# Two bias vectors added to rows in SBUF: by GpSimd instructions, or by accumulating transfers from GpSimd's queue

## The chip, the cores and the metric

One core of one Trainium2 chip runs the kernel, in one launch. The metric is the device time of an execution in microseconds, and a kernel's time is the median over its runs. The engines: TensorE (PE) multiplies matrices, VectorE (DVE) and ScalarE (ACT) do elementwise work, GpSimd (POOL) does some too and issues transfers from a queue of its own, SyncE (SP) issues most transfers. They share an on-chip memory of 128 partitions (SBUF). PE writes its products to eight banks of PSUM. Engines wait for each other by semaphores only.

## The reference

The input x has 64 blocks of 32 rows by 512 columns, float32. Four layers of the form x = x + ffn(cond(x)) follow one another. Cut to what matters here:

```
x = x + ffn0(cond0(x))    # cond: a 32x32 mix for each block; ffn0: silu(gate) * up, then down, 1792 wide
x = x + ffn1(cond1(x))    # cond1: grouped convolution, 9 taps, along the 512 columns
x = x + ffn2(cond2(x))    # top 8 of 64 experts' bias rows, mixed, and the row scaled
x = x + ffn3(cond3(x))    # x * in_scale @ sign(W).T * out_scale + bias, scales from a softmax routing

def ffn1(c):
    combine = top2(softmax(c @ W_router.T))
    lora = einsum(einsum(c, A_stack) * combine, B_stack) * 2
    return c @ W_base.T + b_base + lora

def ffn3(c):
    routing = softmax(c @ gate_w.T)
    return c * (routing @ in_channel_scale) @ sign(weight).T * (routing @ out_channel_scale) + bias
```

The change is about b_base of layer 1 (512 numbers, bbase in the kernel) and bias of layer 3 (512 numbers, bias3). Both are the same for all 2048 rows of x.

## The kernel before

x lives in SBUF as x_all, 128 partitions by 16 tiles of 512 columns. A group g is four tiles (GT = 4), so there are four groups, and each layer runs over groups 0 to 3. Nothing schedules the work: each engine's program is written out by hand, runs in the order of the code, and waits where a wait_ge stands. PE turns a group's tiles into cT (cond), DVE adds the cond's bias, PE multiplies cT by the layer's weights into PSUM banks, and DVE or GpSimd adds the result to x_all.

**Layer 1.** Its convolution needs other rows beside each other, so layer 0's result takes a way through DRAM. GpSimd's part copies each tile into two halves (L446), SP writes them to y_dram (put_back, L316), and SP reads them back as stg, 16 transfers for each group (regroup, L308). PE's conv takes stg, DVE turns and adds (cond1), and PE makes the router's logits and the low-rank product (lora_a_router), then the product with wbase (base), then lora_b. Group 1's conv comes behind group 0's base on PE and waits for group 1's stg. DVE's residual(1, g) adds the four banks to x_all, and ahead of its first addition waits until base_bias(g) is done. base_bias(g) (L457 to L461) is one GpSimd instruction that adds bbase to the four tiles of group g. base_bias(0) stands behind the wait for all 16 parts and for the weights of layer 1; the other three stand behind the splitting of layer 2's and 3's weights (eb_lo, in_w, out_w), in a loop.

**Layer 3.** For each group DVE's route3 makes the routing weights: a multiply into ex, two casts into rcat (L1167), two subtractions into rcat. PE turns rcat (turn_routing, L769) and makes from it the scales (in_scales, out_scales). DVE scales cT, ACT and DVE and GpSimd split it into high and low parts: GpSimd's split_x (L496) makes the even low parts, c_lo or c_lo_odd. PE's sign_product(g, j) takes them. DVE's scale_out multiplies the product by the output scale into t1. GpSimd adds the layer's bias to x_all (bias_3, L499 to L501, one instruction for four tiles) and then t1 (finish_3, L508, one for each tile), and SP stores the tile. GpSimd's order in this layer is block_diagonal(3, 1), split_x(0), bias_3(0), and then for g = 0, 1, 2: block_diagonal(3, g + 2), bias_3(g + 1), three tiles of finish_3(g), split_x(g + 1), the last tile of finish_3(g). bias_3(g) waits until PE has read x_all for cond of group g.

bbase and bias3 come from DRAM as tiles of 128 partitions by 512, issued by SP beside the other weights.

Of the kernel before, what the change touches and what calls it, by code (L numbers as in the profile page):

```python
# [17 lines left out]
ALU = mybir.AluOpType  # L18
# [3 lines left out]
P = 128  # L22
D = 512
# [29 lines left out]
def build(nc, A, out):  # L53
    ctx = ExitStack()
    with ctx:
        def sb(name, shape, dt=F32):
            return ctx.enter_context(nc.sbuf_tensor(name, shape, dt))

        def sem(name):
            return ctx.enter_context(nc.semaphore(name))  # L60
# [65 lines left out]
        with ExitStack() as first:  # L126
            def sb1(name, shape):
                return first.enter_context(nc.sbuf_tensor(name, shape, F32))

            war = sb1("war", [P, S, AR])  # L130
            wbase = sb1("wbase", [P, S, D])
            wlb = sb1("wlb", [P, D])
            bbase = sb1("bbase", [P, D])
            hm = sb1("hm", [P, GT, P])
            hmT = sb1("hmT", [P, TOK])
# [9 lines left out]
        wsg = sb("wsg", [P, S, D])  # L145
        bias3 = sb("bias3", [P, D])
        inc3 = sb("inc3", [P, D])
# [85 lines left out]
        s_hmT = sem("s_hmT")  # L233
        s_base_bias = sem("s_base_bias")

# [27 lines left out]
        s_scaled_lo_odd = sem("s_scaled_lo_odd")  # L263
        s_bias3 = sem("s_bias3")
        s_rescaled = sem("s_rescaled")
# [11 lines left out]
        WLOADS = 16 * 2 * CB * Q  # L277
        LOADS1 = 16 * 10


        @block.sync
        def _(sp):
# [66 lines left out]
            for n in range(4):  # L349
                at, h, to = n * ROWS, n // 2, n % 2  # L350
                rows = slice(h * WIN + to, (h + 1) * WIN, 2)
                for dst, src in ((war, "war"), (wbase, "wbase")):
                    sp.dma_start(dst[at:at + ROWS], A[src][rows]).then_inc(s_weights1, 16)
            for dst, src in ((bbase, "bbase"), (wlb, "wlb")):
                sp.dma_start(dst[:], A[src]).then_inc(s_weights1, 16)
            sp.wait_ge(s_up, G * M)
            for dst, src in ((eb2, "eb2"), (inc3, "inc3"), (outc3, "outc3"), (wsg, "wsg"),
                             (wr2, "wr2"), (rb2, "rb2"), (wr3, "wr3"), (bias3, "bias3")):
                sp.dma_start(dst[:], A[src]).then_inc(s_weights23, 16)
# [19 lines left out]
        def _(pool):  # L379
# [77 lines left out]
            def base_bias(g):  # L457
                pool.wait_ge(s_weights1, LOADS1)
                xg = x_all[:, ds(g * GT, GT), :]
                pool.tensor_tensor(xg, xg, bbase[:].unsqueeze(1).broadcast_to([P, GT, D]),  # L460
                                   ALU.add).then_inc(s_base_bias, 1)  # L461

            pool.wait_ge(s_parted, NT)
            base_bias(0)
            pool.wait_ge(s_weights23, 16 * 8)
            pool.wait_ge(s_w_hi, 4)
            half = P // 2
            pool.wait_ge(s_base_bias, 1)
            pool.tensor_tensor(eb_lo[:], eb2[:], eb_hi[:].bitcast(F32), ALU.subtract).then_inc(s_w_lo, 1)
            pool.wait_ge(s_w_lo, 1)  # L470
            for n, (w, src) in enumerate(((in_w, inc3), (out_w, outc3))):
                pool.tensor_tensor(w[half:P], src[half:P], w[half:P].bitcast(F32), ALU.subtract).then_inc(s_w_lo, 1)
                pool.wait_ge(s_w_lo, n + 2)
            with pool.Fori(1, G) as g:
                base_bias(g)

# [21 lines left out]
            def bias_3(g):  # L498
                pool.wait_ge(s_cond_mm[3], S * (g + 1))  # L499
                xg = x_all[:, g * GT:(g + 1) * GT, :]  # L500
                pool.tensor_tensor(xg, xg, bias3[:].unsqueeze(1).broadcast_to([P, GT, D]), ALU.add).then_inc(s_bias3, 1)  # L501

            def finish_3(g, js):
                pool.wait_ge(s_bias3, g + 1)
                for j in js:
                    pool.wait_ge(s_rescaled, g * GT + j + 1)
                    xg = x_all[:, g * GT + j, :]
                    pool.tensor_tensor(xg, xg, t1[:, j], ALU.add).then_inc(s_x_new[3], 1)  # L508
# [18 lines left out]
        def _(pe):  # L527
# [155 lines left out]
            def layer1(g, more):  # L683
                base(g)
                pe.wait_ge(s_hm, g + 1)
                if more:
                    for q in range(Q - 1):
                        conv(g + 1, q)
                    pe.wait_ge(s_turned1, Q * (g + 1) + 1)
                    turn_hm(g)  # L690
                    conv(g + 1, Q - 1)
                    lora_b(g)
                    lora_a_router(g + 1)
                else:
                    cond(2, 0, SPARING, [nothing, nothing, nothing, lambda: (turn_hm(g), pe.wait_ge(s_cT[2], 1))])
                    lora_b(g)
                    pe.wait_ge(s_w_lo, 3)
                    pe.wait_ge(s_weights23, 16 * 8)
                    router2(0)
                pe.wait_ge(s_x_new[1], GT * (g + 1))  # L700
# [127 lines left out]
        def _(act):  # L828
# [48 lines left out]

            act.wait_ge(s_weights23, 16 * 8)
            act.wait_ge(s_product[0], G * GT)
# [58 lines left out]
        def _(dve):  # L938
# [160 lines left out]
            dve.wait_ge(s_set, 3)  # L1099
            with dve.Fori(0, G - 1) as g:  # L1100
                route1(g)
                cond1(g + 1)
                dve.wait_ge(s_base_bias, g + 1)
                residual(1, g)
            route1(G - 1)
            cond(2, 0, SPARING)
            dve.wait_ge(s_base_bias, G)
            residual(1, G - 1)
# [107 lines left out]

            dve.wait_ge(s_bias3, G)
            dve.wait_ge(s_rescaled, NT)
# [91 lines left out]
```

## Time and profile before

| | |
|---|---|
| median of 3 runs | 581.22 us (581.1 to 581.5) |
| the profiled execution | 581.92 us |
| its span, first to last instruction | 579.9 us |
| mean granted TensorE clock | 0.983 |
| PE busy | 549.5 us, 95% of the span |
| DVE busy | 263.1 us, 45% |
| ACT busy | 134.1 us, 23% |
| GpSimd busy | 186.7 us, 32% |
| moved by DMA | 50.32 MB, mean 87 GB/s |

The profile is one execution. Its page lists busy time by engine, the span in 40 slices, the chain of work that ended last, and groups of instructions by line with what they waited for. The trace behind it can be asked for one engine's timeline, for its waits, and for the busy time of all engines in a stretch of time. Layer 0 takes the time up to about 342 us, layer 1 to about 455, layer 2 to about 505, layer 3 the rest. A granted clock of 1.00 is TensorE's 2.4 GHz, 0.50 is 1.2 GHz. The DMA share of a stretch is the mean busy share of 16 DMA engines; packets of one engine can overlap, so it can pass 1.

### The profile page before, as it was taken

Reading aid. Unit: us, or ns where it says so; the run is one execution under the profiler, and the core shown is the slowest. Engines: PE = TensorE matmul, PEld = TensorE weight load, DVE = VectorE, ACT = ScalarE, POOL = GpSimd, SP = SyncE. Lnnn points to the kernel's source line nnn. Section 1 sums busy time; section 2 is a strip of 40 time slices with the busy share of each in tenths; the row PEclk is TensorE's granted clock in tenths of the full one; section 3 lists DMA queues with packets and bytes.
Section 4 is the critical chain, followed back from the end, with each engine's and each line's share of the span. In section 5 each row is a group of like instructions: output and inputs, shape, how many; then the busy total and the mean of one; then the engine's idle time right before and its main releaser. Section 6 shows DMA issues by size and latency. Waiting matters only on the chain.

```text
span 579.9 us, 7213 instructions
## 1 busy us (share of the span) xinstructions
PE 549.5 (95%) x2689; PEld 421.6 (73%) x2689; DVE 263.1 (45%) x529; ACT 134.1 (23%) x230; POOL 186.7 (32%) x152
## 2 busy tenths in 40 slices
PE   7999999999999999999999998699999999886996
PEld 5788888888888888888888863254455889764774
DVE  4542254522227222245222264435262687767775
ACT  4322223222223222232222221101010132232232
POOL 2699981200002100012000008600000155466986
PEclk9999999999999999999999999699999999997999
DMA  9398230490000400003050059494910343110412
GB/s 303 134 419 312 50 93 0 107 176 24 0 0 32 131 0 0 0 0 92 1 128 1 0 193 172 65 144 57 178 18 1 90 114 86 19 18 1 139 62 109
DMA packets 84211, 50.32 MB, mean 87 GB/s; under 512 B 69600, under 2 KB 74464, under 8 KB 83424
## 3 DMA queue, kind: packets, MB, share of 16 engines
q1 hardware_dynamic: 82096, 38.97, 30.8%
q0 software_dynamic: 2016, 11.01, 5.3%
q8 instruction: 12, 0.20, 0.1%
q10 hardware_dynamic: 80, 0.08, 0.0%
q14 instruction: 7, 0.06, 0.0%
HBM read 31.93 MB, written 8.62 MB: 70 GB/s over the span
## 4 chain that ended last, share of the span: by engine, by line
PE 82%; DVE 9%; DMA 4%; SPq 2%; issue 2%; POOL 1%; ACT 1%; DVEq 0%; POOLq 0%
PE ps L529 80%; DMA xs<-in_x 2%; SPq L308 2%; DVE cT L940 1%; DVE rcat L1167 1%; DMA stg<-y_dram 1%; POOL x_all L483 1%; DVE rest L1122 1%; DVE x_all L940 1%; DMA y_dram<-prod 1%; PE ps L769 1%; DVE lg L940 1%; DVE c_lo L940 0%; DVE ex L940 0%; DVE t L940 0%
## 5 line engine op out<-in xcount | busy, mean ns | idle before, releaser
L529 PE MATMUL ps<-c_lo,wl 128*128 128x512 f32 x448 | 172.9, 390 | 0.4 <-POOL c_lo L408 0.3
L529 PE MATMUL ps<-c_hi,wl 128*128 128x512 f32 x448 | 173.1, 390 | 0.2
L940 DVE TENSOR_TENSOR hff<-silu,ps 128x512 f32<-128x512 f32 x56 | 38.5, 688 | 163.2 <-PE ps L529 163.1
L529 PEld LDWEIGHTS ps<-c_lo,wl 128*128 128x128 f32 x448 | 84.1, 188 | 18.6 <-POOL c_lo L408 0.7
L529 PEld LDWEIGHTS ps<-c_hi,wl 128*128 128x128 f32 x448 | 84.1, 188 | 18.1 <-ACT c_hi L830 0.8
L529 PE MATMUL ps<-wl,h_hi 128*128 128x512 f32 x224 | 87.7, 391 | 0.0
L529 PE MATMUL ps<-wl,h_lo 128*128 128x512 f32 x224 | 87.2, 389 | 0.0
L940 DVE TENSOR_TENSOR h_lo<-hff,h_hi 128x512 fp32r<-128x512 f32 x56 | 46.1, 823 | 39.1 <-ACT h_hi L830 39.1
L408 POOL TENSOR_TENSOR c_lo<-cT,c_hi 128x512 fp32r<-128x512 f32 x8 | 10.7, 1343 | 158.1 <-ACT c_hi L830 158.1
L830 ACT ACTIVATE h_hi<-hff 128x512 fp32r<-128x512 f32 x56 | 35.4, 632 | 112.5 <-DVE hff L940 112.5
L864 ACT ACTIVATE silu<-ps 128x512 f32<-128x512 f32 x56 | 33.5, 598 | 116.4 <-PE ps L529 116.4
L529 PE MATMUL ps<-wbase,cT 128*128 128x512 f32 x128 | 55.6, 592 | 0.0
L529 PEld LDWEIGHTS ps<-wl,h_hi 128*128 128x128 f32 x224 | 42.1, 188 | 10.4 <-issue 1.7
L529 PEld LDWEIGHTS ps<-wl,h_lo 128*128 128x128 f32 x224 | 42.1, 188 | 8.6
L529 PEld LDWEIGHTS ps<-wbase,cT 128*128 128x128 f32 x128 | 24.0, 190 | 28.7 <-issue 28.7
L940 DVE TENSOR_TENSOR cT<-ps,bias_bc 128x512 f32<-128x512 f32 x48 | 31.3, 684 | 19.4 <-PE ps L529 19.1
L446 POOL COPY prod<-x_all 128x512 f32<-128x512 f32 x16 | 10.1, 647 | 92.9 <-DVE x_all L940 84.8
L416 POOL TENSOR_TENSOR blk<-agg,pack_c 128x512 f32<-128x512 f32 x11 | 11.4, 1041 | 78.3 <-PE ps L529 78.3
L529 PEld LDWEIGHTS ps<-blk,xs 128*128 128x128 f32 x256 | 31.5, 201 | 3.1 <-DMA xs<-in_x 1.8
L529 PE MATMUL ps<-blk,xs 128*128 128x128 f32 x256 | 32.7, 286 | 0.2 <-DMA xs<-in_x 0.2
L483 POOL TENSOR_TENSOR x_all<-x_all,t 128x512 f32 (+1 forms) x16 | 20.0, 1285 | 29.7 <-ACT t L895 29.7
L991 DVE STREAM_TRANSPOSE tr<-ps 128x512 f32<-128x512 f32 x16 | 11.3, 712 | 36.6 <-PE ps L529 36.5
(155 smaller groups left out, 651.5 us busy)
## 6 DMA issues: line engine op xcount, KB each, us to landing
wl<-in_wl POOLq DMA_DIRECT2D x14, 768.0 KB, 10.0
stg<-y_dram SPq DMA_DIRECT2D x64, 128.0 KB, 4.9
xs<-in_x SPq DMA_DIRECT2D x4, 1024.0 KB, 7.9
x_all<-in_x SPq DMA_DIRECT2D x1, 4096.0 KB, 14.5
y_dram<-prod SPq DMA_DIRECT2D x16, 256.0 KB, 2.3
xs<-x_all SPq DMA_DIRECT2D x4, 1024.0 KB, 4.9
out_x<-x_all SPq DMA_DIRECT2D x16, 256.0 KB, 2.0
bias_bc<-bias_dram SPq DMA_DIRECT2D x15, 256.0 KB, 5.0
```

The source lines that it names most:

```text
L308: sp.dma_start(stg[dt * ROWS:(dt + 1) * ROWS, q, :, at:at + WIN], src.rearrange("b p c -> p b c")).then_inc(s_staged[1], 16)
L408: pool.tensor_tensor(c_lo[:, s], cT[:, s], c_hi[:, s].bitcast(F32), ALU.subtract).then_inc(s_c_lo_even, 1)
L416: pool.tensor_tensor(blk[:].rearrange("p j (b o) -> p j b o", b=TB), agg[:, COND[l], ds(g * GT, GT)].unsqueeze(2).broadcast_to([P, GT, TB, ...
L446: pool.tensor_copy(halves_x[:, j % 2], x_all[:, j, :].rearrange("p (s c h) -> p h s c", s=S, h=2)).then_inc(s_parted, 1)
L483: pool.tensor_tensor(xg, xg, t1[:, j:j + 1, :], ALU.add).then_inc(s_t1_added, 1)
L529: return pe.matmul(o, l, r, start=start, stop=stop)
L769: ins = pe.transpose(bank(5)[:, cols(j)], rcat[:, j], ident)
L830: return act.activation(o, i, ACT.Copy)
L864: act.activation(silu[:, m % 2], bank(4 + 2 * (m % 2)), ACT.Silu).then_inc(s_silu, 1)
L940: return dve.tensor_tensor(o, a, b, op)
L991: dve.transpose(tr[:, q % 2], bank(4 + q)).then_inc(s_turned1, 1)
L1122: ins = dve.match_replace(rest[:, j], m8[:, j], logit[:, j], LOWEST)
```

## The change

base_bias(g) and bias_3(g) become DMA issues on GpSimd's queue. Each reads the bias vector from DRAM, where it lies as 128 rows of 512, repeats it over four tiles, and adds it to x_all in SBUF (accum_op). The SBUF tiles bbase and bias3 go, and so do the loads that filled them. Each of the eight transfers has a semaphore of its own, which rises by 16 when it has landed. All four base_bias are issued in a row once all 16 parts are made, and no longer wait for layer 1's weights. The bias_3 issues stand where the additions stood. DVE's loop over groups of layer 1 is written out, since its wait is for another semaphore in each group; the instructions in it are the same.

```diff
-            bbase = sb1("bbase", [P, D])
-        bias3 = sb("bias3", [P, D])
-        LOADS1 = 16 * 10
+        LOADS1 = 16 * 9
...
             def base_bias(g):
-                pool.wait_ge(s_weights1, LOADS1)
-                xg = x_all[:, ds(g * GT, GT), :]
-                pool.tensor_tensor(xg, xg, bbase[:].unsqueeze(1).broadcast_to([P, GT, D]),
-                                   ALU.add).then_inc(s_base_bias, 1)
+                pool.dma_start(x_all[:, g * GT:(g + 1) * GT, :], A["bbase"].unsqueeze(1).broadcast_to([P, GT, D]),
+                               accum_op=ALU.add).then_inc(s_base_bias[g], 16)
 
             pool.wait_ge(s_parted, NT)
-            base_bias(0)
-            pool.wait_ge(s_weights23, 16 * 8)
+            for g in range(G):
+                base_bias(g)
+            pool.wait_ge(s_weights23, 16 * 7)
             pool.wait_ge(s_w_hi, 4)
             half = P // 2
-            pool.wait_ge(s_base_bias, 1)
...
-            with pool.Fori(1, G) as g:
-                base_bias(g)
...
             def bias_3(g):
                 pool.wait_ge(s_cond_mm[3], S * (g + 1))
-                xg = x_all[:, g * GT:(g + 1) * GT, :]
-                pool.tensor_tensor(xg, xg, bias3[:].unsqueeze(1).broadcast_to([P, GT, D]), ALU.add).then_inc(s_bias3, 1)
+                pool.dma_start(x_all[:, g * GT:(g + 1) * GT, :], A["bias3"].unsqueeze(1).broadcast_to([P, GT, D]),
+                               accum_op=ALU.add).then_inc(s_bias3[g], 16)
 
             def finish_3(g, js):
-                pool.wait_ge(s_bias3, g + 1)
+                pool.wait_ge(s_bias3[g], 16)
...
-            with dve.Fori(0, G - 1) as g:
+            for g in range(G - 1):
                 route1(g)
                 cond1(g + 1)
-                dve.wait_ge(s_base_bias, g + 1)
+                dve.wait_ge(s_base_bias[g], 16)
                 residual(1, g)
```

GpSimd's order at the seam of layers 0 and 1, from its last part of x (COPY) to the loop of layer 2, before the change (the row of L460 behind the branch is in a loop of three):

```order
L446 COPY prod<-x_all 128x512 [waits s_y1]
L460 TENSOR_TENSOR x_all<-x_all,bbase 128x2048 [waits s_weights1,s_parted]
L469 TENSOR_TENSOR eb_lo<-eb,eb_hi 128x512 [waits s_base_bias,s_w_hi,s_weights23]
L472 TENSOR_TENSOR in_w<-inc,in_w 64x512 [waits s_w_lo]
L472 TENSOR_TENSOR out_w<-outc,out_w 64x512 [waits s_w_lo]
L474 UNCONDITIONAL_BRANCH [waits s_w_lo]
L460 ISA [waits s_weights1]
L460 TENSOR_TENSOR x_all<-x_all,bbase 128x2048
```

and after it:

```order
L443 COPY prod<-x_all 128x512 [waits s_y1]
L455 DMA x_all<-in_bbase 128x4x512 [waits s_parted]
L455 DMA x_all<-in_bbase 128x4x512 x3
L464 TENSOR_TENSOR eb_lo<-eb,eb_hi 128x512 [waits s_w_hi,s_weights23]
L467 TENSOR_TENSOR in_w<-inc,in_w 64x512 [waits s_w_lo]
L467 TENSOR_TENSOR out_w<-outc,out_w 64x512 [waits s_w_lo]
```

The three base_bias that came behind the splitting of the weights now come ahead of it, beside the first, and all of them are transfers.

GpSimd's order in layer 3, from the even low parts of group 0 (c_lo) to those of group 1 (c_lo_odd), before the change:

```order
L496 TENSOR_TENSOR c_lo<-cT,c_hi 128x512 [waits s_scaled_hi] x2
L501 TENSOR_TENSOR x_all<-x_all,bias 128x2048 [waits s_cond_mm3]
L416 TENSOR_TENSOR blk<-agg,pack_c 128x512 [waits s_cond_mm3]
L501 TENSOR_TENSOR x_all<-x_all,bias 128x2048 [waits s_cond_mm3]
L508 TENSOR_TENSOR x_all<-x_all,t 128x512 [waits s_rescaled,s_bias3]
L508 TENSOR_TENSOR x_all<-x_all,t 128x512 [waits s_rescaled] x2
L496 TENSOR_TENSOR c_lo_odd<-cT,c_hi_odd 128x512 [waits s_scaled_hi] x2
```

and after it:

```order
L489 TENSOR_TENSOR c_lo<-cT,c_hi 128x512 [waits s_scaled_hi] x2
L493 DMA x_all<-in_bias 128x4x512 [waits s_cond_mm3]
L413 TENSOR_TENSOR blk<-agg,pack_c 128x512 [waits s_cond_mm3]
L493 DMA x_all<-in_bias 128x4x512 [waits s_cond_mm3]
L501 TENSOR_TENSOR x_all<-x_all,t 128x512 [waits s_rescaled,s_bias3_0]
L501 TENSOR_TENSOR x_all<-x_all,t 128x512 [waits s_rescaled] x2
L489 TENSOR_TENSOR c_lo_odd<-cT,c_hi_odd 128x512 [waits s_scaled_hi] x2
```

No row has changed its place here. The two additions of the bias are issues, and the first finishing addition waits for the semaphore of group 0's transfer, where it waited for an instruction of its own engine.

## Rows read from the trace of the kernel before

**Rows 1.** The page's chain that ended last, share of the span by line

```profile
PE ps L529 80%; DMA xs<-in_x 2%; SPq L308 2%; DVE cT L940 1%; DVE rcat L1167 1%; DMA stg<-y_dram 1%; POOL x_all L483 1%; DVE rest L1122 1%; DVE x_all L940 1%; DMA y_dram<-prod 1%; PE ps L769 1%; DVE lg L940 1%; DVE c_lo L940 0%; DVE ex L940 0%; DVE t L940 0%
```

**Rows 2.** PE's waits: who for whom, total us, times, longest us

```profile
PE ps L769 <- DVE rcat L940: 7.8, 4, 5.1
```

**Rows 3.** Timelines of SP and PE, layer 1: start us, us, work [idle before]

```profile
350.51 12.20 SPq L308 DMA_DIRECT2D stg<-y_dram  x16
...
367.33 5.39 PE L529 MATMUL ps<-stg,wconv 128*64 128x512 f32 x12 [7.38 <-DMA stg<-y_dram]
```

**Rows 4.** Timeline of DVE in layer 3, route3 of groups 0, 1 and 2

```profile
508.16 0.19 DVE L940 TENSOR_TENSOR ex<-ex,stat 128x32 f32<-128x32 f32 x1
508.39 0.27 DVE L1167 CAST rcat<-ex 128x32 fp32r<-128x32 f32 x2
508.69 0.42 DVE L940 TENSOR_TENSOR rcat<-ex,rcat 128x32 f32<-128x32 f32 x2
...
520.86 0.72 DVE L940 TENSOR_TENSOR ex<-ex,stat 128x32 f32<-128x32 f32 x1
521.61 4.51 DVE L1167 CAST rcat<-ex 128x32 fp32r<-128x32 f32 x2
526.16 1.36 DVE L940 TENSOR_TENSOR rcat<-ex,rcat 128x32 f32<-128x32 f32 x2
...
543.82 0.79 DVE L940 TENSOR_TENSOR ex<-ex,stat 128x32 f32<-128x32 f32 x1
544.64 1.28 DVE L1167 CAST rcat<-ex 128x32 fp32r<-128x32 f32 x2
```

**Rows 5.** Timeline of GpSimd in layer 3

```profile
515.42 5.11 POOL L501 TENSOR_TENSOR x_all<-x_all,bias 128x2048 f32<-128x2048 f32 x1
...
521.49 4.51 POOL L501 TENSOR_TENSOR x_all<-x_all,bias 128x2048 f32<-128x2048 f32 x1
...
532.29 1.28 POOL L496 TENSOR_TENSOR c_lo_odd<-cT,c_hi_odd 128x512 fp32r<-128x512 f32 x1 [1.59 <-ACT c_hi_odd L830]
...
539.98 4.58 POOL L501 TENSOR_TENSOR x_all<-x_all,bias 128x2048 f32<-128x2048 f32 x1
544.52 1.27 POOL L508 TENSOR_TENSOR x_all<-x_all,t 128x512 f32<-128x512 f32 x1
```

**Rows 6.** Timeline of PE in layer 3

```profile
527.57 1.11 PE L769 MATMUL ps<-pack_c,rcat 128*128 128x128 f32 x4 [5.14 <-DVE rcat L940]
...
539.28 1.08 PE L529 MATMUL ps<-sgn,c_lo_odd 128*128 128x512 f32 x4
...
546.43 0.66 PE L769 MATMUL ps<-pack_c,rcat 128*128 128x128 f32 x4 [1.05 <-DVE rcat L940]
...
561.91 0.66 PE L769 MATMUL ps<-pack_c,rcat 128*128 128x128 f32 x4 [0.32 <-DVE rcat L940]
```

**Rows 7.** Stretches: us, busy us (x) by engine, PEclk, DMA share, GB/s

```profile
527.50:534.80 7.30, 7.14 (x21) 5.51 (x22) 3.59 (x7) 2.42 (x4) 3.78 (x3) 0.60 0.01 2
546.40:551.00 4.60, 4.48 (x20) 3.35 (x21) 3.53 (x6) 2.33 (x4) 3.82 (x3) 1.00 0.42 159
```

**Rows 8.** DMA: x_all's load; xs issued at 73.4; weights; first xs load

```profile
x_all<-in_x SPq DMA_DIRECT2D x1, 4096.0 KB, 14.5
...
DMA to landing us min/median/max: 7.5/7.5/7.5
...
L385 POOL DMA_DIRECT2D wl<-in_wl x2: 541/630/719, 4.7 to 5.4; - x2
...
DMA to landing us min/median/max: 7.6/8.3/9.1
...
2.13 12.12 DMA xs<-in_x
```

**Rows 9.** Line L460, min/median/max ns; then GpSimd's waits

```profile
L460 POOL TENSOR_TENSOR x_all<-x_all,bbase x4: 4492/4508/4546, 350.1 to 368.1; 128x2048 f32 x3, 128x2048 f32<-128x2048 f32 x1
...
POOL blk L416 <- PE ps L529: 78.3, 1, 78.3
```

**Rows 10.** A stretch ahead of group 1's conv (columns as in rows 7)

```profile
362.00:365.00 3.00, 0.00 (x0) 0.00 (x0) 0.00 (x0) 0.00 (x0) 3.00 (x2) 0.62 1.42 149
```

More of the change, by code:

```diff
@@ L233, in build @@
         s_hmT = sem("s_hmT")
-        s_base_bias = sem("s_base_bias")
+        s_base_bias = [sem(f"s_base_bias{g}") for g in range(G)]
         s_w_hi = sem("s_w_hi")
@@ L263, in build @@
         s_scaled_lo_odd = sem("s_scaled_lo_odd")
-        s_bias3 = sem("s_bias3")
+        s_bias3 = [sem(f"s_bias3_{g}") for g in range(G)]
         s_rescaled = sem("s_rescaled")
@@ L353, in _ @@
                     sp.dma_start(dst[at:at + ROWS], A[src][rows]).then_inc(s_weights1, 16)
-            for dst, src in ((bbase, "bbase"), (wlb, "wlb")):
-                sp.dma_start(dst[:], A[src]).then_inc(s_weights1, 16)
+            sp.dma_start(wlb[:], A["wlb"]).then_inc(s_weights1, 16)
             sp.wait_ge(s_up, G * M)
             for dst, src in ((eb2, "eb2"), (inc3, "inc3"), (outc3, "outc3"), (wsg, "wsg"),
-                             (wr2, "wr2"), (rb2, "rb2"), (wr3, "wr3"), (bias3, "bias3")):
+                             (wr2, "wr2"), (rb2, "rb2"), (wr3, "wr3")):
                 sp.dma_start(dst[:], A[src]).then_inc(s_weights23, 16)
@@ L697, in layer1 @@
                     pe.wait_ge(s_w_lo, 3)
-                    pe.wait_ge(s_weights23, 16 * 8)
+                    pe.wait_ge(s_weights23, 16 * 7)
                     router2(0)
@@ L875, in _ @@
             layer0(G - 1, False)
-            act.wait_ge(s_weights23, 16 * 8)
+            act.wait_ge(s_weights23, 16 * 7)
             act.wait_ge(s_product[0], G * GT)
@@ L1106, in _ @@
             cond(2, 0, SPARING)
-            dve.wait_ge(s_base_bias, G)
+            dve.wait_ge(s_base_bias[G - 1], 16)
             residual(1, G - 1)
@@ L1215, in _ @@
             scale_out(G - 1, range(GT))
-            dve.wait_ge(s_bias3, G)
+            dve.wait_ge(s_bias3[G - 1], 16)
             dve.wait_ge(s_rescaled, NT)
```

## The prediction

> **What bounds the kernel now.** Read the chain of work that ended last first: PE's matmuls hold 80% of it and no DMA or GpSimd line is above 2% [rows 1]. So an edit to GpSimd and DMA counts only where PE stands idle. Then ask where PE waits. Two waits matter for this change. In layer 3 PE waits 7.8 us in four places for rcat, the routing weights that DVE writes, and 5.1 us of that in one place [rows 2]. At the start of layer 1's second group (group 1) it waits 7.38 us for stg, the regrouped rows that SP's transfers bring from DRAM, 16 of which were issued in 12.20 us [rows 3].
>
> **Why the long wait for rcat.** Set DVE's rows of layer 3 beside GpSimd's [rows 4, 5]. The same small steps run once for each group. In group 0 the multiply takes 0.19 us, the two casts 0.27, the two subtractions 0.42. In group 1 they take 0.72, 4.51 and 1.36: 5.71 us more. GpSimd's addition of bias3 to four tiles runs from 521.49 for 4.51 us, exactly over the casts. In group 2 the multiply and the casts take 0.79 and 1.28, 1.61 us more. GpSimd's addition of 539.98 to 544.56 lies on the first, and the finishing addition right behind it (1.27 us) on the second. Without the long one the finishing addition comes some 4 us earlier, ahead of DVE's steps. So I read the two engines as taking turns. The additions held DVE's work back.
>
> **Layer 3, what goes.** The four additions of 4.51 to 5.11 us leave GpSimd and its place is taken by four DMA issues. PE's waits are 5.14, 1.05 and 0.32 us in groups 1, 2 and 3 [rows 6]. The first two are shorter than what DVE gets back (5.71 and 1.61). The third I count with them, as the same kind of collision. That is 6.51 us. What is left of the 7.8 us, 1.3 us in group 0, has nothing of GpSimd in it (DVE's steps are the short ones there) and stays. The clock comes on top. After the 5.14 us of idling PE's granted clock is 0.60 over the stretch from the routing turn to the next cond product. The same stretch of group 2, whose wait was only 1.05 us, has 1.00 and lasts 4.6 us instead of 7.3 [rows 7]. Without the long wait those 2.7 us go too, unless some other gap lets the clock fall. Layer 3's upper bound is 6.5 + 2.7 = 9.2 us.
>
> **Layer 3, what comes.** Now finish_3(0), GpSimd's addition of t1 to group 0's rows, must wait until a transfer has landed. Queued behind it on GpSimd is split_x(1), which makes the even low parts for sign_product(1, 0) on PE, and behind that everything of group 2. Before, PE took the low parts at 539.28 [rows 6]. With 5.14 + 2.70 us gone it would want them at 531.4, and the second even one some 0.5 us later. GpSimd has to do three finishing additions of 1.27 us and two splittings of 1.28 first [rows 5], 6.4 us, so the bias must be there by 525.5. The issue is made when the additions' place comes, at 515.42 [rows 5]. So there are 10.1 us from issue to landing. The trace has no accumulating transfer. The nearest rows are an xs load of 1024 KB, the same size in rows of the same 2 KB, at 7.5 us, and x_all's load of 4096 KB at 14.5 us, 3.6 us for each megabyte [rows 8]. If the transfer costs no more than such a load it is in time and nothing is lost. If its destination's bytes must be read as well, it takes 7.5 + 3.6 = 11.1 us and is 1.0 us late. Each further microsecond costs one. I take 11.1, since adding to a row can't be done without reading it. Layer 3 then gives 9.2 - 1.0 = 8.2 us. In groups 1 to 3 the transfer is issued some 15 us ahead of its user, enough for either price. An issue itself costs GpSimd 0.54 to 0.72 us in the weight loads, which have 128 rows each [rows 8]. These have 512, so four times 0.6, 2.4 us, is the upper bound, below the 4.5 us that it replaces.
>
> **Layer 1, what goes.** Four additions of 4.5 us [rows 9], none on the chain: behind them GpSimd is idle for 78 us. The load of bbase and that of bias3 (256 KB each) go from SP's queue where nobody waits. The loop of layer 1 on DVE is written out, which moves no work. I cost these at nothing. The cover is the long product with wbase, during which DVE has finished its routing.
>
> **Layer 1, what comes.** All four transfers, 4096 KB, are now issued in a row the moment that the last part of x is parted, at 350 us. That is the moment at which SP starts the 16 stg transfers [rows 3] for which PE waits. These don't leave the DMA engines free: between 362 and 365 us their busy share is 1.42 (the times of packets overlap within an engine, so it can pass 1) at only 149 GB/s, with PE at a standstill and its clock falling [rows 10]. So the new bytes are added to the wait, not hidden. The price of 4096 KB in rows of 2 KB, read and written once, is x_all's 14.5 us [rows 8]. The lower bound is nothing, if the accumulating queue is served only when stg's leaves gaps. The upper bound is 29 us, if a row must be read twice and all of it goes ahead of stg. Two thoughts lead to the same middle. With the bytes priced once and all in stg's way it is 14.5. With the bytes priced twice, but the queues served in turn, stg's stretch of some 14 us doubles, which is 14 again. I take 14.5. The trace does show two queues sharing: the first xs load, with three weight loads of GpSimd's queue beside it, took 12.12 us instead of 7.5 [rows 8]. That is 4.6 us for the two slices of 768 KB that had landed by then or within 0.3 us of it, 3.1 us for each megabyte, near x_all's 3.6. For the later groups nothing is left over: their stg transfers are issued only after group 1's conv, and each bias has more time than the one before it.
>
> What an accumulating row costs no row here shows. The Trainium skill, page Collectives: The Full Stack (section The bandwidth ceiling: the fold count and why AG ≠ RS ≠ AR), says that a transfer that adds on its way reads two sources for each byte that it writes, and so delivers half as fast as a copy. By that rule with all of it in stg's way the sum would be that of the second rival.
>
> **The sum.** 581.2 + 14.5 - 8.2 = 587.5 us. The profiled execution took 581.92 us with a span of 579.9, 0.7 and -1.3 us from the median. The difference above is one of terms, and I add it to the median.
>
> **Rivals.**
> 1. *Faster.* Stg isn't held back: the accumulating transfers are slow each for itself, with their rows in flight while the engines serve SP's queue. Then layer 1 costs 0 to 7 us and layer 3 gives 8.2 to 9.2. Around 2.5 us of cost the time is 581.2 + 2.5 - 9 = 574.7. For it: the trace shows no accumulating row, and packets of one engine can overlap. Against it: the xs row, and stg's busy share. It decides from a layer 1 cost below 7 us.
> 2. *The reading of the destination counts fully* (the rule of the Trainium skill's collectives page is this one). Rows are read twice, in stg's way all the while: 29 us. 581.2 + 29 - 8.2 = 602.0. For it: a stg row is 256 B and the new rows are 2 KB, so serving in turn by rows gives stg the smaller part.
> 3. *The adding itself is slow*, beyond twice a load. Then layer 3's first bias is late as well, and the time is above 608.
> 4. *They cancel.* Layer 1 costs within 1.2 us of layer 3's gain: about 581.
>
> **Chances.** Forecast (layer 1 costs 9.5 to 20 us) 0.40, rival 1 0.25, rival 2 0.19, rival 3 0.10, rival 4 0.06. A measurement of this kernel tells about 0.2%, 1.2 us, from no change. Faster is rival 1, 0.25. The same is rival 4, 0.06. Slower is the rest, 0.69. The range runs from 573.5, which holds nearly all of rival 1, to 608, which holds rival 2: it leaves out the first's far end and rival 3, some 0.15. The forecast's own range is 582.5 to 593.
>
> **What would show it.** PE's wait for stg at group 1 of layer 1, 7.38 us before, should be near 22; near 8 is rival 1, 36 is rival 2. DMA's GB/s between 351 and 380 gives the rate. DVE's casts of rcat in group 1 should be back at 0.3 us and PE's wait there gone, with the granted clock at 1.0 through layer 3. GpSimd's wait ahead of finish_3(0) should end near 526. The reason for the gain falls if rcat's casts stay long without GpSimd's additions, and the sum falls if accumulating transfers go at another rate than loads, which no row here prices.

## The result, and the profile after

| | before | after |
|---|---|---|
| median | 581.16 us (577.17 to 581.5, 4 runs) | 592.27 us (592.16 to 595.04, 4 runs) |
| the profiled execution | 581.92 us | 592.16 us |
| its span | 579.9 us | 590.2 us |
| mean granted TensorE clock | 0.983 | 0.976 |
| GpSimd busy | 186.7 us | 160.4 us |
| moved by DMA | 50.32 MB | 58.18 MB |

The changed kernel takes 1.022 times as long (95% interval 1.017 to 1.027): 11.1 us slower. The forecast was 587.5 us, 6.3 us slower. The sign is right, and the loss is nearly twice the one forecast.

The page of after: busy time, the DMA packets, and the chain that ended last by engine. GpSimd has lost 26 us of work and PE's share of the chain is 80% where it was 82%, and that of SP's queue has gone from 2% to 5%.

```profile
PE 544.2 (92%) x2689; PEld 418.7 (71%) x2689; DVE 250.9 (43%) x529; ACT 134.1 (23%) x230; POOL 160.4 (27%) x152
...
DMA packets 88147, 58.18 MB, mean 99 GB/s; under 512 B 69696, under 2 KB 74560, under 8 KB 87360
...
PE 80%; DVE 6%; SPq 5%; DMA 4%; issue 2%; POOL 2%; ACT 1%; DVEq 0%; POOLq 0%
```

Next the waits of after: who for whom, total us, times, longest us. The wait for rcat answers to [rows 2].

```profile
PE ps L522 <- DMA stg<-y_dram: 28.7, 1, 28.7
PE ps L522 <- DVE cT L933: 2.0, 3, 0.9
PE ps L762 <- DVE rcat L933: 1.3, 1, 1.3
...
POOL x_all L501 <- DMA x_all<-in_bias: 5.4, 1, 5.4
```

Two things have moved. PE's wait for rcat went from 7.8 us in four places to 1.3 in one. PE's wait for stg went from 7.38 us to 28.7.

**Layer 1.** The timelines of SP, PE and GpSimd in after answer to [rows 3]. Columns are start, us, work, and in brackets the idle time before it.

```profile
349.09 5.26 POOL L455 DMA_DIRECT2D x_all<-in_bbase  x4 [0.31 <-POOL prod L443]
...
349.27 33.56 SPq L306 DMA_DIRECT2D stg<-y_dram  x16
...
387.28 4.67 PE L522 MATMUL ps<-stg,wconv 128*64 128x512 f32 x12 [28.70 <-DMA stg<-y_dram]
```

The same 16 stg transfers took 12.20 us to issue before and take 33.56 now. The next fences show why: the time of GpSimd's four transfers from issue to landing; the stretch from 359 to 377 us, in which they run; in the same stretch each queue's packets, MB and share of the 16 engines (q0 is GpSimd's queue, q1 is SP's); and a stretch right after.

```profile
L455 POOL DMA_DIRECT2D x_all<-in_bbase x4: 1334/2101/2920, 349.1 to 351.4; - x4
...
DMA to landing us min/median/max: 11.2/18.9/26.7
```

```profile
359.00:377.00 18.00, 0.00 (x0) 0.00 (x0) 0.00 (x0) 0.00 (x0) 0.00 (x0) 0.63 1.13 200
...
q0 software_dynamic: 1599, 3.17, 94.7%
q1 hardware_dynamic: 1742, 0.43, 18.3%
...
380.00:383.00 3.00, 0.00 (x0) 0.00 (x0) 0.00 (x0) 0.00 (x0) 0.00 (x0) 0.50 1.41 149
```

The four landed at 360.3, 366.2, 372.1 and 378.1 us, one every 5.9 us. So 1.05 MB goes in 5.9 us, which is 178 GB/s of the 200 GB/s in the stretch. The packets are the rows: 3.17 MB in 1599 of them is 2 KB each, and 0.43 MB in 1742 is 256 B each. The two queues get about as many rows as each other, and so stg, with its short ones, gets 0.43 MB in 18 us, 24 GB/s. When the last of the four has landed, stg goes at 149 GB/s, its rate of before [rows 10]. PE starts 9.2 us later. In this time SP's queue moves 1.37 MB, of which 0.26 belong to the next load on it, bias_bc. So of stg's 2.10 MB (16 transfers of 128 KB) only some 1.0 had passed in the 29 us before. Every engine stands still in PE's 28.7 us, and PE's clock falls to its lower level, 0.50.

**Layer 3.** Timelines of DVE and GpSimd in after, group 1, answering to [rows 4, 5].

```profile
539.95 0.19 DVE L933 TENSOR_TENSOR ex<-ex,stat 128x32 f32<-128x32 f32 x1
540.18 0.27 DVE L1160 CAST rcat<-ex 128x32 fp32r<-128x32 f32 x2
540.48 0.42 DVE L933 TENSOR_TENSOR rcat<-ex,rcat 128x32 f32<-128x32 f32 x2
...
534.51 1.29 POOL L493 DMA_DIRECT2D x_all<-in_bias  x1
535.33 1.55 POOL L413 TENSOR_TENSOR blk<-agg,pack_c 128x512 f32<-128x512 f32 x1
536.31 1.82 POOL L493 DMA_DIRECT2D x_all<-in_bias  x1
543.53 3.78 POOL L501 TENSOR_TENSOR x_all<-x_all,t 128x512 f32<-128x512 f32 x3 [5.40 <-DMA x_all<-in_bias]
```

The casts take 0.27 us in place of 4.51, and the routing turn on PE follows without a gap. The stretch that answers to the first one of [rows 7], from the turn to the next cond product, shows the clock at 1.00 and 5.05 us where there were 7.30 at 0.60:

```profile
541.35:546.40 5.05, 4.95 (x26) 3.81 (x25) 3.72 (x7) 2.61 (x5) 2.87 (x3) 1.00 1.20 200
```

**By stretches.** The chain in order of time gives marks that exist in each kernel: where layer 0's stretch starts, where the last of layer 2's GpSimd additions start (L476 in after, L483 before), and where the last addition of the program starts.

| | first loads | layers 0 to 2 | layer 3 to the mark |
|---|---|---|---|
| before | 23.65 | 475.93 | 76.89 |
| after | 22.23 | 496.45 | 68.07 |
| difference | -1.4 | +20.5 | -8.8 |

The 1.4 us of the first loads are not the change's: the same loads end between 22.1 and 23.8 us in all kernels below, with or without it. The three differences sum to 10.3, the difference of the spans. The change costs 20.5 us in layer 1 and brings 8.8 in layer 3.

### The profile page after: what moved, and what is told of

Its sections match the earlier page's. It is cut to its first block, busy times and chain, and to the rows that moved or that the text cites. A ratio compares the mean times of both kernels' runs of the same rounds, so it can differ in the third digit from the quotient of the medians.

```text
span 590.2 us, 7128 instructions
## 1 busy us (share of the span) xinstructions
PE 544.2 (92%) x2689; PEld 418.7 (71%) x2689; DVE 250.9 (43%) x529; ACT 134.1 (23%) x230; POOL 160.4 (27%) x152
## 2 busy tenths in 40 slices
DMA packets 88147, 58.18 MB, mean 99 GB/s; under 512 B 69696, under 2 KB 74560, under 8 KB 87360
## 4 chain that ended last, share of the span: by engine, by line
PE 80%; DVE 6%; SPq 5%; DMA 4%; issue 2%; POOL 2%; ACT 1%; DVEq 0%; POOLq 0%
PE ps L522 79%; SPq L306 5%; DMA bias_bc<-bias_dram 2%; DVE cT L933 2%; DMA stg<-y_dram 1%; POOL x_all L476 1%; DMA y_dram<-prod 1%; DVE rest L1115 1%; DVE x_all L933 1%; DMA pack_a<-in_pack_a 0%; DVE c_lo L933 0%; DVE lg L933 0%; PE ps L668 0%; DVE m L1111 0%; DVE t L933 0%
## 5 line engine op out<-in xcount | busy, mean ns | idle before, releaser
L522 PEld LDWEIGHTS ps<-wbase,cT 128*128 128x128 f32 x128 | 24.0, 190 | 28.7 <-issue 28.7
L522 PE MATMUL ps<-stg,wconv 128*64 128x512 f32 x64 | 17.9, 683 | 28.7 <-DMA stg<-y_dram 28.7
L443 POOL COPY prod<-x_all 128x512 f32<-128x512 f32 x16 | 10.1, 650 | 93.0 <-DVE x_all L933 84.8
## 6 DMA issues: line engine op xcount, KB each, us to landing
x_all<-in_bias POOLq DMA_DIRECT2D x4, 1024.0 KB, 10.6
```

Of the source, the lines that this page charges most:

```text
L443: pool.tensor_copy(halves_x[:, j % 2], x_all[:, j, :].rearrange("p (s c h) -> p h s c", s=S, h=2)).then_inc(s_parted, 1)
L522: return pe.matmul(o, l, r, start=start, stop=stop)
```

## Experiments

The theory after this result: the two halves of the change are independent. In layer 3 it frees DVE from GpSimd's long additions. In layer 1 the four transfers hold the DMA engines while stg is wanted, longer than four loads would, by the adding. Each experiment stands beside runs of the kernel before in the same session. Line numbers differ by kernel.

### One half alone: l3_only and l1_only

l3_only has only layer 3's part of the change:

```diff
             def bias_3(g):
                 pool.wait_ge(s_cond_mm[3], S * (g + 1))
-                xg = x_all[:, g * GT:(g + 1) * GT, :]
-                pool.tensor_tensor(xg, xg, bias3[:].unsqueeze(1).broadcast_to([P, GT, D]), ALU.add).then_inc(s_bias3, 1)
+                pool.dma_start(x_all[:, g * GT:(g + 1) * GT, :], A["bias3"].unsqueeze(1).broadcast_to([P, GT, D]),
+                               accum_op=ALU.add).then_inc(s_bias3[g], 16)
...
```

l1_only has only layer 1's part, as in the diff ahead of the prediction.

> Layer 3's part of the change alone; layer 1 is as before. Theory: the two parts add up. After the change layer 3 takes 8.8 us less (from the blk at its start, 523.64 against 504.54, to the last addition, 586.75 against 576.47), so this run takes about 581.2 - 8.8 = 572.4. Rival: part of that gain came from what layer 1 or 2 left behind (clock, transfers done early); then it is above 575.

> Layer 1's part alone; layer 3 is as before. Theory: the four accumulating transfers in the way of stg cost PE's wait of 28.7 us in place of 7.4, some 20 us net, so 601 to 602. Rival: if the parts don't add up, it lies nearer to 592.

l3_only: 571.54 us (570.79 to 572.76), ratio 0.986 (0.983 to 0.989), beside 579.64 for before. l1_only: 601.14 us (600.48 to 602.88), ratio 1.038 (1.034 to 1.042). Their waits, PE's for stg and for rcat, first l3_only and then l1_only:

```profile
PE ps L528 <- DMA stg<-y_dram: 6.7, 1, 6.7
...
PE ps L768 <- DVE rcat L939: 1.3, 1, 1.3
```

```profile
PE ps L523 <- DMA stg<-y_dram: 27.7, 1, 27.7
...
PE ps L763 <- DVE rcat L934: 8.0, 4, 5.3
```

Each kernel has the one wait of after and the other of before. -8.1 and +21.5 on 579.6 make 593.0, and after measured 592.3. The halves add.

### Is it the adding, or the bytes? plain_loads

The kernel before, with its GpSimd additions, and at the place where after issues the four accumulating transfers four plain loads of the same size from the same rows of DRAM, into SBUF that nothing reads:

```diff
             pool.wait_ge(s_parted, NT)
+            for g, dst in enumerate((spare[:, 0], spare[:, 1], extra[:, 0], extra[:, 1])):
+                pool.dma_start(dst, A["bbase"].unsqueeze(1).broadcast_to([P, GT, D])).then_inc(s_plain[g], 16)
             base_bias(0)
...
```

> The kernel before, with four plain loads of the same bytes in the same rows (1024 KB each, rows of 2 KB, the same source) issued where the changed kernel issues its accumulating transfers, into SBUF that nobody reads. Nothing is added by transfers. Theory: an accumulating row costs two loads of that row, 29 us for four where x_all's load took 14.5. Then these four land within some 15 to 18 us and PE's wait for stg grows by about 10 us, to 591. Rival: the adding costs nothing and it is only the sharing of the engines that holds stg back; then the wait grows by 20 as in the changed kernel, to 601.

592.16 us (589.45 to 594.74), ratio 1.020 (1.015 to 1.024). PE's wait, then SP's issues, then a stretch while all of it is under way, with the packets and MB of each queue in it:

```profile
PE ps L539 <- DMA stg<-y_dram: 20.7, 1, 20.7
...
350.16 25.86 SPq L314 DMA_DIRECT2D stg<-y_dram  x16
...
356.00:365.00 9.00, 3.31 (x8) 1.14 (x6) 2.33 (x2) 0.00 (x0) 8.31 (x5) 0.98 1.05 357
...
q0 software_dynamic: 780, 3.01, 94.1%
q1 hardware_dynamic: 818, 0.20, 11.4%
```

With the loads and stg together 357 GB/s move, with the accumulating transfers and stg 200. The last load had landed near 370, the last accumulating transfer at 378. For the same bytes PE waits 13.3 us longer than before with loads and 20 to 21 with adding. So the larger part of layer 1's cost is that 4 MB are moved there at all, and the adding makes it about 1.6 times as large. This is also the measurement of my term of 14.5 us: it was the price of plain loads.

The experiment changes one thing more than the adding. By the count of packets the plain loads went in rows of 4 KB (3.01 MB in 780), the accumulating transfers in rows of 2 KB. So a part of the 1.6 could be the shorter rows. Two stretches say that most of it is not. Accumulating rows of 8 KB go at 207 GB/s (2.48 MB in 12 us, under Longer rows below), and these plain rows of 4 KB at 334. And x_all's load in the kernel before, plain rows of 2 KB with only a small load beside them, moves 3.01 MB in 1468 packets between 50 and 58 us, 376 GB/s. No run has plain rows of 2 KB beside stg.

### One transfer more or less: l1_two

Groups 0 and 1 by accumulating transfer, groups 2 and 3 by GpSimd's additions where they stood; layer 3 as before.

```diff
-            base_bias(0)
+            for g in range(2):
+                pool.dma_start(x_all[:, g * GT:(g + 1) * GT, :], A["bbase"].unsqueeze(1).broadcast_to([P, GT, D]),
+                               accum_op=ALU.add).then_inc(s_base_dma[g], 16)
...
-            with pool.Fori(1, G) as g:
+            with pool.Fori(2, G) as g:
                 base_bias(g)
...
```

> Layer 1's part alone, with accumulating transfers for groups 0 and 1 only; groups 2 and 3 get the GpSimd addition, layer 3 is as before. Theory: what counts is the bytes that the queue puts in stg's way, some 5 us of stg's delay for each of the four transfers: about half of the 21.5 us that four cost, so +10.5 us, 590. Rival: a fixed cost (starting the queue, the first transfer's 11 us to landing) holds the larger part; then it lies above 596.

592.13 us (590.14 to 592.78), ratio 1.019 (1.016 to 1.022), 11.2 us over before where 10.5 was expected. PE's wait for stg and the landings:

```profile
PE ps L531 <- DMA stg<-y_dram: 17.8, 1, 17.8
...
DMA to landing us min/median/max: 10.3/13.0/15.8
```

PE's wait goes 7.4, 17.8, 27.7 us with none, two and four transfers (before, l1_two, l1_only). That is 5.2 and 5.0 us for each. The count from after's rates gives the same: a transfer holds the engines for 5.9 us, in which stg gets 24 GB/s, 0.14 MB, worth 0.9 us at 149 GB/s. 5.9 - 0.9 = 5.0.

### Longer rows: l1_rows8k

If the two queues share row for row, rows of 8 KB should leave stg, with its 256 B rows, still less. The bias lies in DRAM four times over, so that a transfer is 128 rows of 8 KB in place of 512 of 2 KB; layer 3 as before.

```diff
-                pool.dma_start(x_all[:, g * GT:(g + 1) * GT, :], A["bbase"].unsqueeze(1).broadcast_to([P, GT, D]),
+                pool.dma_start(x_all[:, g * GT:(g + 1) * GT, :].rearrange("p j n -> p (j n)"), A["bbase4"],
                                accum_op=ALU.add).then_inc(s_base_bias[g], 16)
...
-        "bbase": everywhere(cols(v["L1_ffn_b_base"])),
+        "bbase4": everywhere(np.tile(cols(v["L1_ffn_b_base"]), GT)),
...
```

> Layer 1's part alone with the bias repeated four times in DRAM, so that each partition's part of a transfer is one row of 8 KB in place of four of 2 KB; layer 3 is as before. The bytes are the same. Theory: each DMA engine serves the two queues row for row (178 GB/s against some 24 GB/s beside each other in the changed kernel is 7.4 to 1, rows of 2 KB against 256 B are 8 to 1). With 8 KB rows stg gets a quarter of the rows in the same time and PE's wait grows by another 2 to 3 us: 603 to 604. Rival: queues share by bytes or by time and not by rows; then it stays at 601, or is faster if a row has a cost of its own.

601.78 us (601.04 to 602.09), ratio 1.036 (1.033 to 1.039), which is the time of l1_only. Its landings, a stretch with the transfers under way with the packets and MB of each queue in it, and a stretch after them:

```profile
DMA to landing us min/median/max: 10.0/16.8/24.7
...
359.00:371.00 12.00, 0.80 (x2) 0.00 (x0) 0.00 (x0) 0.00 (x0) 0.00 (x0) 0.64 1.05 214
...
q0 software_dynamic: 336, 2.48, 99.3%
q1 hardware_dynamic: 336, 0.09, 5.4%
...
374.00:377.00 3.00, 0.00 (x0) 0.00 (x0) 0.00 (x0) 0.00 (x0) 0.00 (x0) 0.50 1.43 147
```

The sharing is as expected: 336 rows of 8 KB against 336 rows of 256 B, and stg gets 0.09 MB in 12 us, 7 GB/s, where it got 24 in after. My expectation of 603 to 604 for the time missed all the same. The transfers are faster, which I had left out: the last lands 24.7 us after its issue, 26.5 in l1_only, and the stretch has 214 GB/s where the same one of after has 200. But by 374 the rate is that of stg alone, and PE starts at 387.3, 13 us later. In these 13 us SP's queue moves 1.93 MB, 0.26 of them bias_bc's, so that some 1.7 of stg's 2.10 MB were still to come. In after it was 1.1 MB, and 9.2 us. Faster transfers and a smaller share for stg cancel. The time came out where the rival had it, and alone it would show nothing. The count of packets rules out the rival's sharing by bytes or by time: the rows are equal in number here, 1599 to 1742 in after, and 780 to 818 in plain_loads.

### Other places: l1_after_stg and all_spread

Two kernels move the transfers of layer 1 without changing them. l1_after_stg is l1_only with the four issues behind the wait for group 1's stg:

```diff
+            pool.wait_ge(s_staged[1], STG * 2)
+            for g in range(G):
+                base_bias(g)
...
```

all_spread has the whole change, with base_bias(0) to base_bias(2) each right behind its group's parts in layer 0, base_bias(3) once all of stg has landed, and layer 3's first transfer ahead of split_x(0):

```diff
                 part(g - 1)
+                base_bias(g - 1)
             block_diagonal(2, 0)
             part(G - 1)
...
+            pool.wait_ge(s_staged[1], STG * G)
+            base_bias(G - 1)
...
             block_diagonal(3, 1)
-            split_x(0)
             bias_3(0)
+            split_x(0)
...
```

> Layer 1's part alone, with the four accumulating transfers issued only when group 1's stg has landed; layer 3 is as before. Theory: 4096 KB of accumulating rows hold the DMA engines for some 29 us wherever they stand. Now they meet group 2's stg (issued at 375, needed by PE at 395), which gets only as many rows as they do, lands near 408, and PE waits some 10 to 13 us there: 591 to 594. Rival, from my prediction: nothing is left over for later groups, since their stg has slack; then the time is 581 to 583.

> All eight accumulating transfers, placed where nothing waits for the DMA engines: base_bias(0), (1), (2) in layer 0, each behind its group's parts, base_bias(3) after group 3's stg has landed, bias_3(0) ahead of split_x(0). Theory: the loss of layer 1 is one of place alone, so PE's wait for stg is back at some 7 us and the time is that of layer 3's part alone, 570 to 572. Rival: accumulating transfers cost something wherever they stand (GpSimd's issues of 1.3 us and more, shared ports, later stg loads of layer 0); then it lies clearly above, 575 or more.

l1_after_stg: 592.29 us (590.59 to 592.89), ratio 1.020 (1.017 to 1.024). Group 1's wait is that of before again, and group 2's conv, which didn't wait before, now does:

```profile
367.00 5.28 PE L524 MATMUL ps<-stg,wconv 128*64 128x512 f32 x12 [7.57 <-DMA stg<-y_dram]
...
405.90 4.64 PE L524 MATMUL ps<-stg,wconv 128*64 128x512 f32 x12 [10.91 <-DMA stg<-y_dram]
```

all_spread: 571.32 us (570.05 to 572.04), ratio 0.984 (0.982 to 0.987). The first bias of layer 1 is issued at 109 us, and PE's waits are those of l3_only:

```profile
109.16 1.34 POOL L440 DMA_DIRECT2D x_all<-in_bbase  x1 [0.31 <-POOL prod L448]
...
PE ps L523 <- DMA stg<-y_dram: 6.7, 1, 6.7
...
PE ps L763 <- DVE rcat L934: 1.3, 1, 1.3
```

All eight transfers move the same bytes as in after, and the 20 us are gone. So the cost of layer 1 is one of place alone. This version beats both kernels. Its layer 3 is that of l3_early, further down, which was measured in the same session and leaves layer 1 as before: 571.85 us. So moving layer 1's additions off GpSimd brings nothing that can be told, as the prediction had it.

### What layer 3's gain consists of: no_bias3, l3_split, l3_early

no_bias3 takes the four bias_3 additions out of before and puts nothing in their place.

```diff
-                xg = x_all[:, g * GT:(g + 1) * GT, :]
-                pool.tensor_tensor(xg, xg, bias3[:].unsqueeze(1).broadcast_to([P, GT, D]), ALU.add).then_inc(s_bias3, 1)
...
```

l3_split leaves the work on GpSimd and cuts each addition into four:

```diff
-                xg = x_all[:, g * GT:(g + 1) * GT, :]
-                pool.tensor_tensor(xg, xg, bias3[:].unsqueeze(1).broadcast_to([P, GT, D]), ALU.add).then_inc(s_bias3, 1)
+                for j in range(GT):
+                    xg = x_all[:, g * GT + j, :]
+                    pool.tensor_tensor(xg, xg, bias3[:], ALU.add).then_inc(s_bias3, 1)
...
```

l3_early is l3_only with bias_3(0) issued ahead of split_x(0), so that finish_3(0) need not wait for it.

```diff
             block_diagonal(3, 1)
-            split_x(0)
             bias_3(0)
+            split_x(0)
```

> The kernel before without the four additions of bias3 in layer 3 (that part of the computation is left out). Theory: the gain of layer 3 is all from GpSimd's additions no longer holding DVE's casts, 5.1 + 1.0 + 0.3 us of PE's waits and 2.7 us of clock: 572, the same as with the accumulating transfers or up to 1 us less, since nothing has to land. Rival: the casts are long for another reason; then PE's wait for rcat stays near 5 us and the time near 581.

> The kernel before, with each of the four additions of bias3 cut into four GpSimd instructions of one tile (128x512, some 1.3 us each); no transfer adds anything. GpSimd's work is the same. Theory: DVE is held for as long as the one GpSimd instruction lasts that it meets. Cut into pieces it can go on between them, but each of its small steps can meet the next piece: five steps at up to 1.3 us, so the casts and their neighbours take 2 to 6 us in group 1 in place of 6.6, and the time is 577 to 581. Rival: what holds DVE is GpSimd's share of the SBUF as such; then the steps stretch as before and nothing changes.

> Layer 3's part alone, with bias_3(0) issued ahead of split_x(0), right behind block_diagonal(3, 1), some 9 us earlier. Theory: it has landed when finish_3(0) is reached, and GpSimd's wait of 5 us there goes; the bias_bc load that now takes 13.4 us shares the engines with one accumulating transfer less. What PE loses there is under 1 us (its wait of 0.8 us for cT at group 2), so 0.5 to 1 us below layer 3's part alone, about 571. Rival: nothing of it is on the chain, no change.

no_bias3: 570.24 us (570.08 to 570.8), ratio 0.984 (0.980 to 0.987). Its casts in group 1, and PE's wait for rcat:

```profile
519.37 0.27 DVE L1164 CAST rcat<-ex 128x32 fp32r<-128x32 f32 x2
...
PE ps L766 <- DVE rcat L937: 1.3, 1, 1.3
```

With the additions gone the casts are short. The additions held them, and nothing else did. Layer 3's length to the mark is 67.0 us here, 68.07 in after and 67.99 in l3_only. So the four transfers with all that hangs on them cost layer 3 about 1 us, and the rest of the additions' harm is won back.

l3_split: 579.32 us (577.27 to 581.34), ratio 0.999 (0.997 to 1.001), no difference that can be told. GpSimd's four pieces in group 1, DVE's casts and subtractions, and PE's wait:

```profile
518.49 2.16 DVE L1168 CAST rcat<-ex 128x32 fp32r<-128x32 f32 x2
519.34 4.95 POOL L502 TENSOR_TENSOR x_all<-x_all,bias 128x512 f32<-128x512 f32 x4
520.69 2.41 DVE L941 TENSOR_TENSOR rcat<-ex,rcat 128x32 f32<-128x32 f32 x2
...
PE ps L770 <- DVE rcat L941: 6.6, 4, 3.3
```

DVE gets in between the pieces, but each of its four small steps then lasts as long as the GpSimd instruction beside it. The first cast, from 518.49, ends with blk (518.34, 1.04 us), and the second cast and the two subtractions take 1.2 to 1.3 us each, as the pieces do. That makes 2.16 and 2.41 us, where the two casts took 4.51 before and the subtractions 1.36. PE's longest wait goes from 5.1 to 3.3 us. Layer 3 is 74.55 us in place of 76.89 in the trace, and of these 2.3 us the timed runs show nothing clear. Cutting finer moves the stall and doesn't remove it.

The Trainium skill, page SBUF — State Buffer (section Who interferes with whom), says that DVE and GpSimd share a pair of ports as an exclusive lock, held for a whole instruction, so that of two instructions which both need it the one that comes second is blocked, not slowed. The trace agrees: 4.51 us of casts under one instruction of 4.51 us, and, with pieces of 1.28 us, two steps in 2.16 and two in 2.41.

l3_early: 571.85 us (569.73 to 572.41), ratio 0.983 (0.981 to 0.986). GpSimd's wait in l3_only, and its place in l3_early:

```profile
523.09 3.78 POOL L507 TENSOR_TENSOR x_all<-x_all,t 128x512 f32<-128x512 f32 x3 [5.37 <-DMA x_all<-in_bias]
```

```profile
505.63 1.32 POOL L499 DMA_DIRECT2D x_all<-in_bias  x1
...
518.14 1.53 POOL L507 TENSOR_TENSOR x_all<-x_all,t 128x512 f32<-128x512 f32 x1
```

GpSimd's wait of 5.4 us is gone. Layer 3 is 67.17 us in place of 67.99, so 0.8 us of the prediction's 1.0 for the late bias can be seen in the trace, and the timed runs can't tell it from nothing. With it the length is that of no_bias3, 67.0.

## Why the prediction was right in sign and short in size

**What bounds the kernel.** Right. GpSimd lost 26 us of work in after and gained nothing by that; both changes of the time are PE's waits.

**The long wait for rcat.** Right, and shown by no_bias3: without the additions the casts take 0.27 us and the three waits of 5.14, 1.05 and 0.32 us [rows 6] are gone. The 1.3 us in group 0 stayed, as said. The clock stayed at 1.00.

**Layer 3's size.** 8.2 us forecast, 8.8 in the trace, 8.1 in l3_only's runs. The upper bound of 9.2 can be set beside no_bias3: 9.9 in the trace, 9.4 in the runs. The transfer of group 0 landed 8.9 us after its issue, where I took 11.1 and allowed 10.1. Even so finish_3(0) waited 5.4 us for it. So by my own deadline nothing was late, and yet l3_early finds 0.8 us. One part of it is in GpSimd's work behind the wait: three finishing additions and two splittings took 7.2 us (from 543.53) where I had counted 6.4. Another is a wait of PE for cT, 0.9 us in after and 0.8 in l3_only, that before, l3_early and no_bias3 don't have. Ahead of it DVE waits 0.3 us for bias_bc, the layer's cond bias, which SP's queue loads beside the new transfers: it took 13.4 us to land, 3.5 before. This is the sharing of layer 1 over again: until it has landed, bias_bc's 0.26 MB take their turns, in 2064 packets, beside the 1056 of two accumulating transfers. The rest stands just ahead of it on DVE: its two splittings into c_lo_odd take 2.95 us (546.60 to 549.55), 2.36 in l3_early. GpSimd's own two, which the late transfer has pushed to 547.28, last 3.42 us beside them, so here the two engines hold each other up again.

```profile
536.43 13.37 DMA bias_bc<-bias_dram
...
DVE cT L933 <- DMA bias_bc<-bias_dram: 0.3, 1, 0.3
```

I had priced only who waits for the new transfers, not which loads lie beside them.

**The issues.** Too low: 1.29 us for each in layer 3, 1.34 in all_spread, where I had 0.6 and an upper bound of 2.4 us for four. It stands in front of nothing that PE wants, so the sum doesn't feel it.

**Layer 1, what goes.** Nothing, as said: all_spread and l3_only agree within 0.3 us.

**Layer 1, what comes.** This is the step that failed. That stg and the new transfers meet and PE stands still meanwhile is as named. The term's size is wrong. I took 14.5 us, and the trace has 20.5, l1_only's runs 21.5. I had two ways to it, and both are wrong.

The first priced the bytes once, as a load. plain_loads shows that such a price was nearly right for loads: 12.5 us by the runs, 13.3 by PE's wait. But the trace had no accumulating row, and the runs put it at 5.9 us for each megabyte against 3.6 for x_all's load [rows 8]. From the first issue to the last landing the four took 29 us, the upper bound, twice 14.5.

The second priced them twice and let the queues take turns in time, so that stg's stretch would double and then be over. Stg didn't get half. It got 24 of 200 GB/s, an eighth: one row of 256 B for each row of 2 KB. I had written down that serving by rows gives stg the smaller part, as evidence for the second rival, and hadn't carried it to its number. By the count of l1_two it is four times 5.0, 20 us. The 29 us are more than that because stg wasn't held all the while. The first accumulating rows move some 2 us after the first issue, and in the whole 29 us stg got 1.0 MB, for which it needed some 7 us before.

**The rivals.** The second one had the right price for the transfers, 29 us, and was too high for the time (602), as not all of it lay in stg's way. What came lies between it and the forecast: 592.3, inside both the range of 573.5 to 608 and the forecast's own, 582.5 to 593. That it lies in the second is luck: layer 1 cost 20.5, outside the 9.5 to 20 that this range was made from, and layer 3 gave 8.8 where 8.2 was taken. The first rival is out: stg was held back. The third is out too: 29 us is twice a load, not beyond. The Trainium skill's page Collectives: The Full Stack (section The bandwidth ceiling: the fold count and why AG ≠ RS ≠ AR) gives its rule, that the add reads two sources and halves the rate, for reduce-scatter. The trace agrees with the half: 29 us against 14.5. By the rates of GpSimd's queue beside stg it is 334 GB/s against 176, a factor of 1.9, and 1.6 against the 207 of 8 KB rows. That a second read is the cause no run here shows.

**For the later groups nothing is left over.** True in after, because all four transfers had landed before group 1's conv. As a rule it is false: l1_after_stg moves them ahead of group 2's stg and loses 11 us there. I had said that each bias has more time, which is true, and not asked what its transfer does to the next stg.

**What would show it.** PE's wait near 22 was forecast; 28.7 is between that and the 36 of the second rival. The three signs of layer 3 (casts, clock, the wait for rcat) came as written; GpSimd's wait ended 8.9 us after the issue, where the forecast had 10.6.

## What to carry to other kernels

Price a transfer that adds into SBUF as two loads, and put it where no transfer that an engine waits for is under way: here the same eight transfers make the kernel 1.6% faster or 2.2% slower by their place alone. If two queues meet, look at the length of their rows, not at their bytes: they were served about row for row, and the one with 2 KB rows left an eighth of the rate to the one with 256 B rows. And when a small step of VectorE takes exactly as long as a GpSimd instruction beside it, it is the GpSimd instruction that has to go or move; cutting it up only spreads the stall.

## What the runs showed of the hardware beyond that

**Issuing costs GpSimd more than the weight loads led me to think.** A plain load of 1024 KB takes it 0.80 us in plain_loads, where it goes in 256 rows of 4 KB, an accumulating one 1.3 us, in 512 rows of 2 KB. The weight loads of 128 rows take 0.54 to 0.72 [rows 8], and the first accumulating transfer of 128 rows in l1_rows8k 0.92. So both the number of rows and the adding seem to cost. The first two of the plain loads:

```profile
L471 POOL DMA_DIRECT2D spare<-in_bbase x2: 778/798/818, 350.0 to 350.8; - x2
```

**The instruction behind an accumulating issue is longer in the record.** Behind the four issues eb_lo's subtraction of 128x512 takes 3.44 us, and blk's takes 1.55 in the fence on layer 3 above. Without issues ahead they take 1.26 and 1.04. Behind the four plain issues of plain_loads the addition of bbase takes 4.55 us, as it does without them. Whether the engine is still writing the transfer's descriptors or it is the trace that counts both, these runs don't tell.

```profile
352.21 3.44 POOL L464 TENSOR_TENSOR eb_lo<-eb,eb_hi 128x512 fp32r<-128x512 f32 x1
```

**Open.** What limits accumulating rows to 176 GB/s in 2 KB rows, where 8 KB rows went at 207, isn't settled; that a destination in SBUF must be read as well is only the nearest reason. That the queues share row for row is counted in the traces, with rows of 2, 4 and 8 KB beside rows of 256 B; no run's time shows it by itself.
